# A two-layer graph transformer on one core: ten and twelve sorted blocks of targets in place of eight and ten, and fewer, wider operations

## The reference

```python
for l in range(L):                                   # L = 2
    xn = _layernorm(x, ln1_g[l], ln1_b[l])           # lax.rsqrt(var + 1e-05)
    deg = ... # count of edges by source, standardized
    pos = xn @ Wpos[l] + bpos[l] + deg[:, None] * Wdeg[l][0] + bdeg[l]
    xp = xn + pos
    q, k, v = xp @ Wq[l] + bq[l], xp @ Wk[l] + bk[l], xp @ Wv[l] + bv[l]   # as (n, H, HD)
    att = jnp.einsum('ehd,ehd->eh', q[dst], k[src]) / scale
    att = jnp.nan_to_num(jnp.clip(att, -50.0, 50.0), ...)
    ex = jnp.exp(att - m[dst])                       # m: largest att of each target
    s = jax.ops.segment_sum(ex, dst, num_segments=n)
    msg = (v[src] * (ex / (s[dst] + 1e-16))[:, :, None]).reshape(-1, D)
    x = x + (jax.ops.segment_sum(msg, dst, num_segments=n) @ Wo[l] + bo[l])
    h = jax.nn.gelu(_layernorm(x, ln2_g[l], ln2_b[l]) @ W1[l] + b1[l], approximate=False)
    x = x + (h @ W2[l] + b2[l])
# outside: x = _layernorm(x_in + x)
```

## Time and profile before

| | |
|---|---|
| timed runs, median of 3 | 3647.36 us (3645.29 to 3647.68) |
| the profiled execution, first to last instruction | 5559.9 us |
| PE busy | 3461.6 us (62%), mean granted clock 0.744 |
| DVE busy | 2916.7 us (52%) |
| POOL busy | 2472.4 us (44%) |
| ACT busy | 1771.1 us (32%) |
| moved by DMA | 548.28 MB, mean 99 GB/s |
| gathers | 1936 + 640 = 2576, mean 954 and 950 ns |

### The profile page before, as it was taken

One profiled execution on the slowest core, in us unless ns is written; L12 is line 12 of the kernel. 1 busy time (PEld: TensorE's weight loads), 2 busy tenths in 40 slices (PEclk: granted clock), 3 DMA queues, 4 the chain that ended last, 5 costly groups with the idle time before them and its releaser, 6 DMA issues.

```text
span 5559.9 us, 72300 instructions
## 1 busy us (share of the span) xinstructions
PE 3461.6 (62%) x24196; PEld 2666.6 (48%) x24475; DVE 2916.7 (52%) x6780; ACT 1771.1 (32%) x4391; POOL 2472.4 (44%) x2597
## 2 busy tenths in 40 slices
PE   5834656655665656666566376666666566666666
PEld 4623445444454445444444254455555455545545
DVE  9944545554454545555455354554554454545455
ACT  2301232323333332323234133333333333333334
POOL 1065444444444444444542544445444454444443
PEclk7756777777777777777777677777777777777777
DMA  2133333333333333333332333333333333333332
GB/s 73 49 111 87 88 106 93 102 88 95 102 94 99 94 102 89 104 95 96 107 105 65 106 103 109 108 107 113 96 108 106 108 110 113 111 102 115 109 104 73
DMA packets 404556, 548.28 MB, mean 99 GB/s; under 512 B 78348, under 2 KB 318656, under 8 KB 403988
## 3 DMA queue, kind: packets, MB, share of 16 engines
q0 software_dynamic: 123648, 337.81, 20.9%
q1 hardware_dynamic: 273030, 198.56, 11.9%
q10 hardware_dynamic: 7506, 7.20, 0.4%
HBM read 518.00 MB, written 25.29 MB: 98 GB/s over the span
## 4 chain that ended last, share of the span: by engine, by line
PE 32%; another core or an unknown queue 30%; DVE 14%; issue 12%; ACT 10%; DVEq 0%; SPq 0%; DMA 0%; ACTq 0%
PE psum L952 7%; PE psum L993 4%; PE psum L1009 3%; ACT scratch L1227 3%; PE psum L1042 3%; PE psum L1026 3%; DVE att L1685 2%; PE psum L970 2%; ACT arena L1238 2%; DVE scratch L1676 2%; DVE kv_ring L1394 1%; PE psum L1123 1%; DVE work L1377 1%; DVE scratch L1700 1%
## 5 line engine op out<-in xcount | busy, mean ns | idle before, releaser
L1971 POOL DMA_INDIRECT kv_ring<-kv_table,src_idx x1936 | 1846.4, 954 | 2132.8 <-DVE scratch L1700 1501.1
L1227 ACT ACTIVATE scratch<-psum 128x512 f32<-128x512 f32 x1148 | 649.5, 570 | 2061.3 <-remote 1442.0
L952 PE MATMUL psum<-arena 128*128 128x256 f32 x1764 | 631.5, 486 | 464.2 <-issue 194.2
L1971 POOL DMA_INDIRECT arena<-kv_table,src_idx x640 | 607.8, 950 | 664.6 <-DVE scratch L1700 489.7
L1726 DVE SCALAR_TENSOR_TENSOR arena<-psum,in_block,arena 128x136 f32 x644 | 200.9, 353 | 1286.4 <-remote 1187.3
L993 PE MATMUL psum<-q_win,scratch 64*128 64x128 f32 x5152 | 534.3, 349 | 285.7 <-issue 149.9
L952 PEld LDWEIGHTS psum<-arena 128*128 128x128 f32 x1764 | 372.6, 236 | 621.0 <-issue 319.2
L1009 PE MATMUL psum<-scratch 128*64 128x136 f32 x5152 | 519.1, 330 | 185.4 <-issue 154.2
L993 PEld LDWEIGHTS psum<-q_win,scratch 64*128 64x128 f32 x5152 | 443.2, 243 | 343.1 <-issue 332.5
L1238 ACT COPY arena<-psum 128x512 f32<-128x512 f32 x504 | 265.1, 532 | 986.9 <-remote 524.7
L1685 DVE TENSOR_REDUCE att<-scratch 128x64 f32<-128x1024 f32 (+1 forms) x448 | 525.1, 1172 | 0.1
(11 more groups left out here) (251 smaller groups left out, 4873.9 us busy)
## 6 DMA issues: line engine op xcount, KB each, us to landing
arena<-kv_table SPq DMA_DIRECT2D x126, 896.0 KB
kv_ring<-kv_table,src_idx POOLq DMA_INDIRECT x1936
q_win<-q_table SPq DMA_DIRECT2D x644, 32.0 KB
work<-kv_table SPq DMA_DIRECT2D x98, 128.0 KB
arena<-kv_table,src_idx POOLq DMA_INDIRECT x640
q_win<-q_table SPq DMA_DIRECT2D x126, 64.0 KB
work<-q_table SPq DMA_DIRECT2D x98, 64.0 KB
kv_table<-work SPq DMA_DIRECT2D x49, 128.0 KB
```

Source lines behind the costliest of these rows:

```text
L952: mm = e.matmul(to[:, t % 2 * 2 * D:(t % 2 + 1) * 2 * D], hot_source[:, t * P:(t + 1) * P], source_rows[:, t, :], start=True, stop=True)
L1227: e.activation(to[:, at:at + width], apart[k % 2][:, 0:width], ACT.Relu, bias=1.0, scale=-1.0).then_inc(apart_read, 1)
L1971: e.indirect_dma_start(kv[m % RING_KV][:, t, :], None, kv_table[l], bass.IndirectOffsetOnAxis(ap=src_idx[:, c * T + t:c * T + t + 1], axis ...
```

## The change

- `NBS` becomes 10, 12: layer 0 gets 157 chunks and 70 blocks, layer 1 149 chunks and 84 blocks. There are twelve sorts (ten in layer 0, two in layer 1). Two blocks may now stand two units apart.
- The accumulator ring gets 16 rows (`RING_W`, `AHEAD`), which makes room for a second buffer of block rows; ACT's copies into it wait for the messages two blocks back and not one.
- The queries are multiplied by the keys in one operation a unit, over both banks of `q_edge`, which waits for both halves of the spread.
- The Newton step takes two operations on DVE; the factor -0.5 (var + eps) is made by ACT, ahead of the exponential.
- The next bias row is added by TensorE (a product of a row of ones with the row `b_next`, ahead of `col @ w_qkv`), and DVE then adds the degree's share and writes the row in one operation.
- The sort's rank is reduced straight into bf16.

```diff
-NBS = 8, 10
+NBS = 10, 12
-RING_W = 32
-AHEAD = 8
+RING_W = 16
+AHEAD = 4
...
-        kv_block = part_of(TB * 2 * D).rearrange("p (t d) -> p t d", t=TB)
+        kv_blocks = [part_of(TB * 2 * D).rearrange("p (t d) -> p t d", t=TB) for _ in range(2)]
...
+        q_edges = psum[:, 0:2, :].rearrange("p b n -> p (b n)")
...
-                e.matmul(ps[:, 0:QKV], col, w_qkv[:, l + 1, :], start=True, stop=True).then_inc(done, 1)
+                e.matmul(ps[:, 0:QKV], ones[0:1, :], b_next[0:1, :], start=True, stop=False)
+                e.matmul(ps[:, 0:QKV], col, w_qkv[:, l + 1, :], start=False, stop=True).then_inc(done, 1)
...
-            if m >= 1 and i == 0:
-                e.wait_ge(msg_ready, block_unit(m - 1) + 1)
+            if m >= 2 and i == 0:
+                e.wait_ge(msg_ready, block_unit(m - 2) + 1)
...
             e.activation(tiny[:, 8:9], tiny[:, 7:8], ACT.Ln, bias=small[:, 0:1]).then_inc(norm_log, 1)
+            e.activation(tiny[:, 10:11], tiny[:, 7:8], ACT.Identity, scale=-0.5, bias=small[:, 1:2])
...
-            for h in range(2):
-                f = 2 * n + h
-                ts = part_tiles(l, u, h)
-                rows = slice(ts[0], ts[-1] + 1)
-                e.wait_ge(spread, f + 1)
...
-                    e.wait_ge(apart_read, fill(n, "rows", 2 * h + 1) + 1)
...
+            ts = LAYERS[l].tiles_of(u)
...
+                e.wait_ge(apart_read, fill(n, "rows", 3) + 1)
+                keys = kv_blocks[m % 2][:, 0:ts, 0:D]
+            e.wait_ge(spread, 2 * n + 2)
+            e.tensor_tensor(prod[:, 0:ts * P].rearrange("p (t d) -> p t d", d=D),
+                            q_edges[:, 0:ts * P].rearrange("p (t d) -> p t d", d=D), keys, ALU.mult
+                            ).then_inc(prod_ready, 2)
...
-                    e.tensor_reduce(whole, s_sel.rearrange("p b g -> p g b"), AX_X, ALU.add).then_inc(sort_picked, 1)
-                    e.wait_ge(sort_picked, 3 * (SA * s + q) + 2)
-                    e.tensor_copy(by_run(s_rank)[:, q], whole).then_inc(sort_picked, 1)
+                        e.tensor_reduce(by_run(s_rank)[:, q], s_sel.rearrange("p b g -> p g b"), AX_X, ALU.add
+                                        ).then_inc(sort_picked, 1)
...
-            step(e.scalar_tensor_tensor, out=t, in0=v, scalar=EPS, in1=y, op0=ALU.add, op1=ALU.mult)
-            step(e.scalar_tensor_tensor, out=t, in0=t, scalar=-0.5, in1=y, op0=ALU.mult, op1=ALU.mult)
+            step(e.scalar_tensor_tensor, out=t, in0=y, scalar=minus_half, in1=y, op0=ALU.mult, op1=ALU.mult)
             step(e.scalar_tensor_tensor, out=y, in0=t, scalar=1.5, in1=y, op0=ALU.add, op1=ALU.mult)
...
-                e.scalar_tensor_tensor(out=qkv, in0=wz_next[:], scalar=deg_z[:, j:j + 1], in1=b_next[:], op0=ALU.mult,
-                                       op1=ALU.add).then_inc(deg_row, 1)
...
-                e.tensor_tensor(qkv, ps("qkv")[:, 0:QKV], qkv, ALU.add).then_inc(qkv_ready, 1)
+                e.scalar_tensor_tensor(out=qkv, in0=wz_next[:], scalar=deg_z[:, j:j + 1], in1=ps("qkv")[:, 0:QKV],
+                                       op0=ALU.mult, op1=ALU.add).then_inc(qkv_ready, 1)
```

More of the change, by code:

```diff
@@ L1769, in sort_vector @@
                 elif k == 8 + 3 * q and q < SA:
[L1770 to L1774 removed]
+                    e.wait_ge(sort_picked, 2 * (SA * s + q) + 1)
+                    with nc.allow_low_precision(reason="one of the terms is a whole number up to 128, the others are 0"):
+                        e.tensor_reduce(by_run(s_rank)[:, q], s_sel.rearrange("p b g -> p g b"), AX_X, ALU.add
+                                        ).then_inc(sort_picked, 1)
                 elif k == 9 + 3 * q and q < SA:
[L1776 removed]
+                    e.wait_ge(sort_picked, 2 * (SA * s + q) + 2)
                     if SA * s + q:
```

45 lines of the change are left out of this document (18 added, 27 removed).

## The result

The changed kernel takes 3970.02 us (median of 4 runs, 3959.51 to 3982.19) against 3646.32 us for the kernel before in the same comparison (3644.02 to 3647.68): ratio 1.0892, 95% interval 1.0867 to 1.0917. It is slower by 9%.

A forecast was written before the change was run, and what follows sets the result against it. GpSimd's gathers, issued nearly without pause, were taken as the bound: 3647.4 - 160 (128 fewer gathers) + 4 (degree counting) = 3491, + 31 waits = 3522, + 2 for layer 1's end = 3524 us; range 3465 to 3670.

The forecast's parts named there:

- the term for GpSimd's waits: Behind chunk 17 of layer 0, TensorE and DVE sometimes hold GpSimd: 0 to 156 us, taken as +31.
- The prediction's own sign for this: A timed run at or over 3640 us would say that TensorE or DVE, not GpSimd, had been the bound.
- GpSimd's chain bounds the kernel before: GpSimd issues gathers nearly without pause, one in 1.25 us; TensorE, DVE and ACT keep up behind it.
- the sum of 3633.8: GpSimd's gathers of both layers laid end to end without waits for DVE: 3633.8 us, 13.6 us under the timed median.
- Against: GpSimd's chain would have to meet the median by accident: Argument against TensorE as the bound: GpSimd's chain reaches the timed time within 0.4%.
- the slower rival: Rival: TensorE takes the bound because its clock stays at 0.77; 3964 us, chance 0.15.
- 93 to 95%: Share of TensorE and DVE in the 1400 us behind the first 17 chunks of layer 0, after the change.
- 5.7 us a unit: Pace of two units where TensorE ran freely behind a stop: 5.7 us, against 6.7 needed in layer 0.
- I take these stops for a cost of recording: Idle stretches near 2026 us in the profile, waiting for TensorE, come from recording its many instructions; timed runs have none.
- Products in one operation: On DVE, one operation for the query products saves 90 ns a unit, -41 us.
- I take nothing: DVE's wait for both halves of the query spread on blocks: 0 us, +108 if TensorE were always late.
- Newton, bias row, rank, ring, second buffer: Newton -37 on DVE, +45 on ACT; bias row -27 to -30 on DVE, +32 on TensorE; rank -8; others 0 us.

The follow-up runs named there:

- e8: The kernel before with `NBS = 6, 8`: 3784.93 us, ratio 1.0369.
- e1: The kernel before, unchanged and recorded once more: recorded span 3651.5 us, timed median 3651.65 us.
- e4: The kernel before with only `NBS = 10, 12`, the ring of 16, `AHEAD = 4` and the second buffer of block rows: 3928.11 us, ratio 1.0752.
- e18: e4 with both clips of the scores on DVE left out: 3818.49 us, ratio 1.0468.
- e5: e4 with three of seven tiles' rows products on TensorE left out: 3835.37 us, ratio 1.0515.
- e13: The kernel before with exponentials in SBUF, on a chip where the kernel before takes 5482.74 us: 5337.15 us, ratio 0.9760.
- e16: The kernel before without the clips, on a chip where the kernel before takes 5482.74 us: 5469.96 us, ratio 0.9971.
- e3: The changed kernel with the query products in two operations again: 3924.56 us, ratio 1.0734.
- e10: The changed kernel with `NBS = 8, 10` and the query products in two operations: 3659.81 us, ratio 1.0009.
- e6: e4 with ACT copying only half of the rows (256 of 512 columns): 3876.82 us, ratio 1.0617.
- e7: e4 with `NBS = 9, 11`: 3713.64 us, ratio 1.0182.
- e9: e4 with a third fill bank and the exponentials in SBUF: 3799.63 us, ratio 1.0384.
- e11: The changed kernel with `NBS = 9, 11`, products in two operations, third fill bank and exponentials in SBUF: 3737.91 us, ratio 1.0210.
- e17: e4 with the exponentials in SBUF and still two fill banks: 3941.88 us, ratio 1.0808.

## Why the prediction was wrong

The step that failed is the term for GpSimd's waits, +31 us with 156 as its upper end. It rested on reading the share of each other engine against 100%, and on putting aside that another chain could be level with GpSimd's. The runs show 470 us of added waits in its place, because TensorE, ACT and DVE together were already at their pace in the kernel before. The prediction's own sign for this, a timed run at or over 3640, is what came.

- *GpSimd's chain bounds the kernel before.* Right as the frame, as e8 and the ledger bear out, but only just. That the sum of 3633.8 came within 0.4% was partly luck. Against e1 it left out the holds (28 us beyond their 0.3 us of issue), 21 us because the mean pace is 1.258 and not 1.25 us, and 7 us at the start; it had 25 us too much at the gap between the layers and 13 behind the last gather, both from the record with stops.
- *"Against: GpSimd's chain would have to meet the median by accident"*, the argument that put aside the slower rival. This step failed in substance. That one chain fits the time says that it is hardly held, and nothing of how near the next one is. Here the other was level with it: TensorE's loop already ran at 0.785 of full speed in layer 1 and keeps 0.764 when it sets the pace itself.
- *The holds.* The prediction bounded them by the gain, 0 to 156 us, and took 31. Measured: 506 - 36 = 470. "All that was gained" is no upper end for a wait: past the crossing the other chain's growth counts in full.
- *The capacity behind "93 to 95%".* The shares were right: TensorE's work in layer 0 (busy time by granted clock) is near 1370 us for 1360 predicted, DVE's busy time 1363 for 1360, and in layer 1 1241 for 1235. But 95% was held against 100%, and in the same 1000 us of layer 1 TensorE reaches 0.76 to 0.80 of full speed in the kernels whose pace the loop sets with all its work in place (0.764 in the changed kernel, 0.78 in e4, 0.80 in e18 without the clips). It is no fixed limit: with work taken from TensorE (e5) it is 0.73. The evidence for 5.7 us a unit was two units behind a stop; that all buffers were full there is a likely reason for its being too short, and not shown.
- *Slower, 3964 us.* The right place by the wrong road, so the match is luck. Behind 335 us its work and effective speed came out (2671 us at 0.737, measured 2672 at 0.738), but it made them of a clock of 0.77 with 4.5% of waits, and the clock there is 0.90 with 18% of waits. The row at 0.77 came from the record with stops. The Trainium skill ("TensorE: Matmul & The Clock Gate", section "Why this matters for your kernels") ties full speed to the absence of long idle gaps; the trace agrees in direction (0.93 without the stops, 0.77 with them), and it did not help the forecast, since waits and not the clock were the loss.
- *"I take these stops for a cost of recording".* Wrong: e1 was recorded too and has none; the timed runs of e13 to e16's chip are as long as the record with stops.
- *Products in one operation.* Its DVE term was mis-sized the safe way (predicted -90 ns, measured 1219 in place of 2 x 684, -149 ns). "I take nothing" for the wait on both halves failed: it costs some 58 us at ten and twelve blocks (1.0892 less 1.0734, two comparisons, each with its own kernel before), inside the 108 named as the worst end. DVE's waits for L1026 at its products are 110.6 us against 67.4 in e3.
- *Newton, bias row, rank, ring, second buffer.* Most sizes were right: ACT's new operation takes 281 ns, within 0.16 to 0.43, 27 us go from DVE with the bias row, and TensorE gets 47 us of busy time for it in e3, within 65. Newton's step in two brings DVE 20 us and not 31, since one operation takes 187 ns in place of 159. Together they bring 0, as in e10. An estimate by the rates of e5, e6 and e18 says why: DVE loses 57 us with the rank's copy, TensorE gets 47 and ACT 55, so -0.60 x 57 + 0.47 x 47 + 0.44 x 55 = +12 us.

## What to carry to other kernels

When a chain of one engine explains the time, look next for the pace that the others keep when *they* are waited for, and take that and not 100% as their capacity: here 0.76 to 0.80 of full speed for TensorE in layer 1. It belongs to this loop and its hand-overs and has to be measured anew for another. A change that trades work from the bounding engine to the others is worth its gain only up to the crossing, and past it costs the whole growth of the other chain: the blocks lost 277 us here where 160 were to be gained. Try half the step first (e7) and one step back (e8), which brackets the crossing with two runs. Before reading the clock or idle time from a record whose span is far from the timed median, take another record.

## What the runs showed of the hardware

- A DVE operation with both operands in SBUF holds up GpSimd's gathers. Median gather 0.949 us in e9 as ever (0.946 in e1), but the slowest twentieth 1.67 us and more; mean 1.03 (e9), 1.02 (e11), 1.01 (e17) in place of 0.957, with L1701 at 1215 ns itself hardly longer than with the exponentials in PSUM (1208). Of e9's 267 gathers over 1.2 us, 246 overlap an L1701 in the trace (of all 2448 gathers, 692 do); e1 has 34 such long gathers in all. The Trainium skill, "SBUF — State Buffer", section "Who interferes with whom", says that a DVE instruction with two SBUF inputs contends with a GpSimd instruction that reads SBUF, and these rows agree. Here one operand in PSUM, as in e4, is a way round it.
- Taking work from TensorE lowered its clock (e5, 0.882 to 0.854; a matmul of L952 431 to 468 ns) and so gave part of the gain back.
- Chips differ: the same kernel took 3647 to 3658 us in four comparisons and 5483 on another chip, where TensorE's loads waited some 1800 us in e16 for nothing that the profile shows (some 500 in e1).
